# The factors of the last layer norm's last two batches: from POOL's power to ACT's square root with a Heron step on DVE, and the last batch scaled by DVE

## The reference

```
def _layernorm(x, axis=-1, eps=1e-05):
    m = jnp.mean(x, axis=axis, keepdims=True)
    v = jnp.var(x, axis=axis, keepdims=True)
    return (x - m) / jnp.sqrt(v + eps)

x = _layernorm(x + attention(x))
x = _layernorm(x + clip(x + moe(x), -100, 100))     # the change is in this norm
```

## Time and profile before

| | |
|---|---|
| median of 3 runs | 480.27 us (479.36 to 481.34) |
| the profiled execution's own time | 484.16 us |
| its span, first to last instruction | 482.4 us |
| last stage, first load of results to the end | about 446.8 to 482.4 us |
| ACT's scaling of batches 4 to 7 | 471.12 to 477.38 us |

### The profile page before, as it was taken

The page is one execution under the profiler, slowest core; times in us unless marked ns, Lnnn a source line. Parts: engine busy times, 40 slices in busy tenths (PEclk is TensorE's granted clock), DMA queues, the critical chain, the costliest instruction groups (busy, mean ns, idle before and its releaser), DMA issues.

```text
span 482.4 us, 20473 instructions
## 1 busy us (share of the span) xinstructions
PE 404.3 (84%) x8282; PEld 264.5 (55%) x8282; DVE 374.5 (78%) x995; ACT 326.8 (68%) x778; POOL 278.3 (58%) x443
## 2 busy tenths in 40 slices
PE   8598999899999998998999889789588988794860
PEld 2354446445455555545545545337487877693760
DVE  7887669989999999999998999877977665630381
ACT  5175675786886877777787667675788887770055
POOL 7022332535746747656655666786777777777173
PEclk9989899999999999999999999999799999997995
DMA  6648378745455365265264241133444433320753
GB/s 186 170 119 251 104 233 243 204 143 148 114 168 167 96 182 167 86 196 168 86 195 148 81 124 49 32 85 103 118 131 107 111 95 88 86 76 22 225 190 109
DMA packets 77500, 65.18 MB, mean 135 GB/s; under 512 B 12102, under 2 KB 71757, under 8 KB 77408
## 3 DMA queue, kind: packets, MB, share of 16 engines
q1 hardware_dynamic: 68240, 55.01, 39.1%
q0 software_dynamic: 4512, 8.54, 5.5%
q10 hardware_dynamic: 4656, 0.34, 0.7%
HBM read 36.88 MB, written 25.46 MB: 129 GB/s over the span
## 4 chain that ended last, share of the span: by engine, by line
PE 34%; ACT 18%; DVE 16%; DMA 12%; issue 8%; POOL 5%; SPq 4%; ACTq 3%; POOLq 0%; DVEq 0%
ACT probs L808 11%; PE psum L1038 10%; PE psum L951 10%; DVE nmax L1351 8%; PE psum L985 5%; POOL o_dram L759 4%; DMA o_dram<-probs,xs 4%; DMA experts<-o_dram 3%; DMA xs<-xs_dram 3%; ACTq L853 2%; PE psum L1210 2%; PE psum L1193 2%; ACT k L820 2%; DMA qst<-nmrows 2%; SPq L421 1%
## 5 line engine op out<-in xcount | busy, mean ns | idle before, releaser
L808 ACT ACTIVATE probs<-psum 128x512 f32<-128x512 f32 x320 | 180.3, 598 | 58.6 <-PE psum L951 47.4
L1351 DVE TENSOR_REDUCE nmax<-psum 128x2 f32<-128x1024 f32 (+7 forms) x256 | 181.4, 748 | 25.6 <-PE psum L998 25.2
L691 POOL TENSOR_SCALAR_AFFINE_SELECT probs<-probs 128x512 f32<-128x512 f32 x186 | 84.3, 484 | 113.1 <-ACT probs L808 112.4
L951 PE MATMUL psum<-qst,kst 128*32 128x512 bf16 (+3 forms) x2048 | 121.8, 303 | 18.8 <-ACT probs L808 14.3
L985 PE MATMUL psum<-kst,qst 128*32 128x512 bf16 (+7 forms) x2048 | 99.7, 290 | 4.1 <-DVE nmax L1351 2.6
L759 POOL DMA_INDIRECT o_dram<-probs,xs x77 | 78.2, 1016 | 26.5 <-issue 18.6
L951 PEld LDWEIGHTS psum<-qst,kst 128*32 128x32 bf16 x2048 | 44.0, 96 | 78.7 <-ACT probs L808 58.6
L1038 PE MATMUL psum<-probs,vst 128*32 128x512 f32 (+3 forms) x1024 | 80.9, 436 | 0.0
L998 PE MATMUL psum<-bmask,bident 128*32 128x64 bf16 (+2 forms) x1280 | 66.0, 200 | 1.0 <-issue 1.0
L985 PEld LDWEIGHTS psum<-kst,qst 128*32 128x32 bf16 x2048 | 47.2, 97 | 21.9 <-DVE nmax L1351 4.7
L998 PEld LDWEIGHTS psum<-bmask,bident 128*32 128x32 bf16 x1280 | 35.1, 98 | 14.8 <-issue 1.5
(11 more groups left out here) (221 smaller groups left out, 655.4 us busy)
## 6 DMA issues: line engine op xcount, KB each, us to landing
kst<-dk SPq DMA_DIRECT2D x62, 128.0 KB, 2.9
qst<-dq SPq DMA_DIRECT2D x31, 256.0 KB, 3.6
xs<-xs_dram SPq DMA_DIRECT2D x77, 66.0 KB, 1.9
experts<-o_dram SPq DMA_DIRECT2D x7, 512.0 KB, 4.7
dk<-k SPq DMA_DIRECT2D x7, 384.0 KB, 3.7
dq<-q SPq DMA_DIRECT2D x7, 384.0 KB, 2.7
xT_sb<-in_xT SPq DMA_DIRECT2D x8, 256.0 KB
xTv_sb<-in_xT SPq DMA_DIRECT2D x8, 256.0 KB, 3.7
```

The lines of the kernel that those rows point to most:

```text
L691: pool.affine_select(out=view, in_=view, compare_op=ALU.is_ge, fill=0.0, base=0, pattern=[[0, view.shape[1]], [1, P]], channel_multiplier= ...
L808: act.activation(probs[:, c % 2, p, kk * T:(kk + 1) * T], ps_t[:, k % 2, :], ACT.Exp, scale=SCALE).then_inc(S["exp_done"], 1)
L951: last = pe.matmul(out[32 * g:32 * g + 32], stationary[:, 32 * g:32 * g + 32], moving, skip_group_check=True, **flags)
L1351: last = dve.tensor_reduce(nmax[:, c, 2 * t:2 * t + 2], ps[:, :, at:at + TWO * (t + 1)], AX.X, ALU.max, negate=True)
```

## The change

The batches 6 and 7 (`LEFT = 2`) leave POOL's table `SPREADS`. Their factors are made together, for 8 numbers in each partition. With v = variance + eps, DVE writes v / 4 (`fin_var`), ACT takes its square root r (`fin_root`), and DVE does one Heron step for the square root of v: `fin_std` = (v / 4) / r + r, with a reciprocal and a product for the quotient. A second reciprocal gives `fin_rs`, and one more instruction `fin_off`. ACT then scales batch 6 as before, and DVE scales batch 7 with 4 `tensor_scalar` instructions. SP stores both batches in halves, in the order 7 first half, 6 first half, 7 second half, 6 second half. An activation with the square root on one column is added ahead of the last stage. Some semaphores are merged (`fin_moments` for `fin_stats` and `fin_aggr`, `fin_terms` for `fin_rstd`), and `fin_ready` now rises at every activation.

```diff
--- before.py
+++ after.py
@@ -47,6 +47,7 @@
 
     B1_AT, W2_AT, B2_AT, WCOLS = F, F + FC, 2 * F + FC, 2 * F + FC + D
     FIN = 4
+    LEFT, LINKS = 2, 6
     NT = NTOK * TOPK // P + E - 1
 
 
@@ -204,6 +205,11 @@
         fin_st = sb("fin_st", [P, 2, NQ, 6])
 
         fin_mv = sb("fin_mv", [P, 4, NQ, 2])
+        fin_root = sb("fin_root", [P, LEFT, NQ])
+        fin_var = sb("fin_var", [P, LEFT, NQ])
+        fin_inv = sb("fin_inv", [P, LEFT, NQ])
+        fin_quot = sb("fin_quot", [P, LEFT, NQ])
+        fin_std = sb("fin_std", [P, LEFT, NQ])
         fin_rs = sb("fin_rs", [P, 4, NQ])
         fin_off = sb("fin_off", [P, 4, NQ])
 
@@ -227,7 +233,7 @@
             top_link hot_ready rank_link pos_ready slot_ready
             gate_exp first_link tab_link free_known tables_ready padded gate_link 
             xsT_filled xsT_copied w_copied h_filled gelu_done y_filled y_copied
-            diag_ready summed clipped residual_pool residual_dve fin_stats fin_aggr fin_terms fin_rstd fin_off
+            diag_ready summed clipped residual_pool residual_dve fin_moments fin_terms fin_off fin_rooted fin_last
             fin_ready
             """.split()}
         ITEMS = ("ot", "q", "k", "va", "vb", "on", "woa", "wob", "rk")
@@ -390,7 +396,7 @@
         DVE_AHEAD = 4
 
 
-        SPREADS = ((0, 1), (2, 3), (4, 5), (6,), (7,))
+        SPREADS = ((0, 1), (2, 3), (4, 5))
         POOL_ADDS = {0: 0, 2: 0, 4: 1}
         TAIL_STEPS = {"pe": 12, "act": 12, "dve": 13}
         TABLE_STEP = 13
@@ -603,13 +609,15 @@
 
                     sp.wait_ge(o_loaded[q - 2], 16)
                 load_results(q, range(NQ), o_loaded[q])
-            for q in range(B - 1):
-                sp.wait_ge(S["fin_ready"], 2 * q + 2)
+            for q in range(B - LEFT):
+                sp.wait_ge(S["fin_ready"], NQ * (q + 1))
                 store_results(q, range(NQ))
             for half in range(2):
-                sp.wait_ge(S["fin_ready"], 2 * (B - 1) + half + 1)
+                sp.wait_ge(S["fin_last"], LINKS + 2 * half + 2)
                 store_results(B - 1, (2 * half, 2 * half + 1))
-            sp.wait_ge(out_stored, 16 * (B + 1))
+                sp.wait_ge(S["fin_ready"], NQ * (B - 2) + 2 * half + 2)
+                store_results(B - 2, (2 * half, 2 * half + 1))
+            sp.wait_ge(out_stored, 16 * (B + 2))
 
 
         @block.gpsimd
@@ -773,17 +781,17 @@
             def spread(n):
                 these = SPREADS[n]
                 at, count = these[0] % 4, len(these)
-                pool.wait_ge(S["fin_aggr"], NQ * (these[-1] + 1))
+                pool.wait_ge(S["fin_moments"], 2 * NQ * (these[-1] + 1))
                 if these[0] >= 4:
 
-                    pool.wait_ge(S["fin_ready"], 2 * (these[-1] - 3))
+                    pool.wait_ge(S["fin_ready"], NQ * (these[-1] - 3))
                 rs, off, mv_of = (t[:, at:at + count] for t in (fin_rs, fin_off, fin_mv))
                 pool.tensor_scalar(rs, mv_of[:, :, :, 1], EPS, None, ALU.add).then_inc(S["fin_terms"], 1)
                 pool.tensor_scalar(off, mv_of[:, :, :, 0], -1.0, None, ALU.mult).then_inc(S["fin_terms"], 1)
-                pool.wait_ge(S["fin_terms"], 2 * n + 2)
+                pool.wait_ge(S["fin_terms"], 3 * n + 2)
                 pool.tensor_tensor(rs, rs, mhalf[:].unsqueeze(1).to_broadcast([P, count, NQ]), ALU.pow
-                                   ).then_inc(S["fin_rstd"], 1)
-                pool.wait_ge(S["fin_rstd"], n + 1)
+                                   ).then_inc(S["fin_terms"], 1)
+                pool.wait_ge(S["fin_terms"], 3 * n + 3)
                 pool.tensor_tensor(off, off, rs, ALU.mult).then_inc(S["fin_off"], 1)
 
             for n in range(len(SPREADS)):
@@ -933,14 +941,22 @@
                 if DIAG_FROM <= j < DIAG_FROM + B * TOPK * NQ:
                     diagonal(j - DIAG_FROM)
 
-            for q in range(B):
+            act.activation(fin_root[:, 0, 0:1], k_ones[:], ACT.Sqrt)
+
+            def scale_rows(q, rows):
+                for n in rows:
+                    at = xr[:, q * T + P * n:q * T + P * n + P]
+                    act.activation(at, at, ACT.Identity, bias=fin_off[:, q % 4, n:n + 1], scale=fin_rs[:, q % 4, n:n + 1]
+                                   ).then_inc(S["fin_ready"], 1)
+
+            for q in range(B - LEFT):
                 act.wait_ge(S["fin_off"], 1 + [q in these for these in SPREADS].index(True))
-                for n in range(NQ):
-                    rows = xr[:, q * T + P * n:q * T + P * n + P]
-                    last = act.activation(rows, rows, ACT.Identity, bias=fin_off[:, q % 4, n:n + 1],
-                                          scale=fin_rs[:, q % 4, n:n + 1])
-                    if n % 2:
-                        last.then_inc(S["fin_ready"], 1)
+                scale_rows(q, range(NQ))
+                if q == B - LEFT - 1:
+                    act.wait_ge(S["fin_last"], 1)
+                    act.activation(fin_root[:], fin_var[:], ACT.Sqrt).then_inc(S["fin_rooted"], 1)
+            act.wait_ge(S["fin_last"], LINKS)
+            scale_rows(B - 2, range(NQ))
 
 
         @block.tensor
@@ -1712,18 +1728,37 @@
                     else:
                         dve.wait_ge(S["residual_dve"], g + 1 - sum(p < g for p in POOL_ADDS))
                     if g >= 2:
-                        dve.wait_ge(S["fin_aggr"], NQ * (g - 1))
+                        dve.wait_ge(S["fin_moments"], 2 * NQ * (g - 1))
                     for n in range(NQ):
-                        dve.bn_stats(fin_st[:, g % 2, n, :], xr[:, g * T + P * n:g * T + P * n + P]).then_inc(S["fin_stats"], 1)
+                        dve.bn_stats(fin_st[:, g % 2, n, :], xr[:, g * T + P * n:g * T + P * n + P]).then_inc(S["fin_moments"], 1)
                     if g >= 4:
 
                         dve.wait_ge(S["fin_off"], 1 + [g - 4 in these for these in SPREADS].index(True))
                     for n in range(NQ):
-                        dve.wait_ge(S["fin_stats"], NQ * g + n + 1)
-                        dve.bn_aggr(fin_mv[:, g % 4, n, :], fin_st[:, g % 2, n, :]).then_inc(S["fin_aggr"], 1)
+                        dve.wait_ge(S["fin_moments"], 2 * NQ * g + n + 1)
+                        dve.bn_aggr(fin_mv[:, g % 4, n, :], fin_st[:, g % 2, n, :]).then_inc(S["fin_moments"], 1)
                 if q < B and q not in POOL_ADDS:
                     dve.wait_ge(S["clipped"], q + 1)
                     dve.tensor_tensor(rows, rows, fin[:, q % FIN, :], ALU.add).then_inc(S["residual_dve"], 1)
+
+            dve.wait_ge(S["fin_moments"], 2 * NQ * B)
+            two = slice((B - LEFT) % 4, (B - LEFT) % 4 + LEFT)
+            dve.tensor_scalar(fin_var[:], fin_mv[:, two, :, 1], 0.25, EPS / 4, ALU.mult, ALU.add).then_inc(S["fin_last"], 1)
+            dve.wait_ge(S["fin_rooted"], 1)
+            link = linker(S["fin_last"], 1)
+            link(dve.reciprocal(fin_inv[:], fin_root[:]))
+            link(dve.tensor_tensor(fin_quot[:], fin_var[:], fin_inv[:], ALU.mult))
+            link(dve.tensor_tensor(fin_std[:], fin_quot[:], fin_root[:], ALU.add))
+
+            dve.wait_ge(S["fin_ready"], NQ * (B - 4))
+            link(dve.reciprocal(fin_rs[:, two], fin_std[:]))
+            link(dve.scalar_tensor_tensor(out=fin_off[:, two], in0=fin_mv[:, two, :, 0], scalar=-1.0, in1=fin_rs[:, two],
+                                          op0=ALU.mult, op1=ALU.mult))
+            q = B - 1
+            for n in range(NQ):
+                rows = xr[:, q * T + P * n:q * T + P * n + P]
+                dve.tensor_scalar(rows, rows, fin_rs[:, q % 4, n:n + 1], fin_off[:, q % 4, n:n + 1], ALU.mult, ALU.add
+                                  ).then_inc(S["fin_last"], 1)
 
 
 # ---- launch: one core; the host transposes weights and activations, nothing else ----
```

## The result

The change makes the kernel 0.5% faster: the median of 20 runs went from 480.37 to 477.87 us, the ratio is 0.9947 (95% interval 0.9929 to 0.9965). One of the 20 executions of the changed kernel took 1343.9 us and is left out of the ratio. The prediction said 480.2 us and no change, so 2.5 us are to be explained.

What follows compares the result with a forecast made beforehand. The prediction took ACT's activations as the bound of the last stage. Its terms, -1.54 + 1.37 + 0.11 = -0.06 us, turned 480.27 into 480.2 us, no change, with a range of 479.1 to 481.4 us.

Steps and rivals of the forecast that it cites:

- The step that failed: End of the span, behind the last store's landing: 3.2 us, with SP waiting 2.9 us, taken as fixed and untouched.
- The removal is worth nothing by itself: POOL's last two factor calls go; batch 7's were ready 0.60 us before ACT needed them, so no gain.
- ACT's count: Last stage on ACT: four activations of batch 7 go at 0.385 us each, 1.54 us less.
- the round trip: Batch 6's factors from ACT's square root through DVE and back to ACT: 1.37 us, between 1.20 and 1.82.
- The stores: Four 128 KB halves at the end: SP's extra issuing hidden by 0.01 us, last store held up 0.11 us by bytes.
- DVE's scaling: Batch 7's four instructions on DVE, at most 0.28 us each, end near 476.6 us, hidden ahead of ACT's batch 6.
- The table load: One new 1.28 us load behind ACT's last GELU, hidden in 30.26 us of ACT idle time.
- The rivals: Last stage: short round trip, 480.0 us (0.20); long one, up to 480.65 us (0.22); table loads inside it, 482.8 us (0.02).
- something unseen: Unnamed causes anywhere, chance 0.06, half on each side and not all of it beyond 0.5%.

Runs made afterwards that it cites:

- e5_before_drain: Kernel before the change plus one POOL DRAIN behind its last indirect DMA, ahead of the last stage; ratio 0.9953, 477.33 against 480.49 us.
- e1_late_pool: Changed kernel plus a one-column POOL memset at its end that waits for DVE's last factor; ratio to the kernel before 1.001, 480.73 against 480.49 us.
- e4_act_queue: Changed kernel with the last half of batch 6 stored from ACT's queue instead of SP's; profile only, 18.0 us from last load's issue to end.
- e6_after_drain: Changed kernel plus the same early POOL DRAIN ahead of the last stage; ratio to the kernel before 0.9948, 478.26 against 480.33 us.

## Why the prediction was wrong

**The step that failed** is in its first part: "From 479.2 to the end of the span at 482.4 us there are 3.2 us, in which SP waits for the other engines' end (2.9 us)", and then "The change touches none of that, and I take it as fixed." The row was read, its size was right, and the question what SP waited for was not asked. It was for POOL's DRAIN, which ended 7.0 us behind the end of POOL's last instruction in all eight profiles without an early DRAIN, and the change moves that instruction: from 475.14 - 462.0 = 13.1 us behind the mark to 468.45 - 459.3 = 9.2 us. Of the 3.2 us, 2.7 were to be had: without the DRAIN the span would have ended 0.4 us behind the landing at 479.3 us, and e5_before_drain came to 17.8 us from the mark in place of 20.4.

**"The removal is worth nothing by itself"** (POOL's two last calls) is wrong for the same reason. That POOL's factors were ready 0.60 us before ACT came to them was right, but POOL had a second customer, the end of the program. The removal is the only part of the change that gains: e5_before_drain has the gain without the rest, e1_late_pool has the rest without the gain.

**ACT's count and the round trip** were right. The saving of 1.54 us was paid back by 1.31 us. The small instructions measured 203 ns (reciprocal, forecast 0.20), 168 and 166 (products, 0.16), 166 (`fin_off`, 0.165) and 191 (square root, 0.20). The Trainium skill's figures ("VectorE: DVE Perf Modes", under the fixed hardware budget) had led to an estimate of 0.15 us for the reciprocal; the trace says 0.203, so between 8 and 32 columns it grows by (353 - 203) / 24 = 6.3 ns a column and not by 8.3. The measurement decides.

**The stores** were under-charged. Forecast: 0.11 us late. The last landing came 476.9 - 474.53 = 2.4 us behind ACT's end, and 1.8 us before: 0.55 us more. SP has a part in it: of four issues in a row the last three cost it 0.469 to 0.492 us each, not 0.372, and the last one began 0.44 us behind ACT, where 0.02 was forecast. The row of that issue in the changed kernel:

```profile
L601 SPq DMA_DIRECT2D out<-xr x1: 492/492/492, 475.0 to 475.0; - x1
...
DMA to landing us min/median/max: 2.0/2.0/2.0
```

The bytes were slower as well: the four halves moved at 249 GB/s, not 296, as this stretch shows (the last three numbers are PEclk, DMA share, GB/s):

```profile
474.40:476.50 2.10, 0.00 (x0) 0.00 (x0) 0.00 (x0) 0.12 (x1) 0.00 (x0) 0.50 0.86 249
```

The engines weren't full in it (0.86), and a half of 131 KB every 0.53 us, which is how SP issued the last ones, is 247 GB/s too, so this rate can be SP's doing. But e4_act_queue took SP's lateness at the last store away, and the landing still came 2.3 us behind ACT's end. How the 0.55 us divide between SP and the bytes isn't shown. So without the drain the change is 1.54 - 1.31 - 0.55 = -0.3 us, a small loss, in keeping with what e6_after_drain (18.0) against e5_before_drain (17.8) shows. The forecast of about nothing for the parts that it looked at was right in kind; DVE's scaling (0.34 us an instruction, one every 0.26 us, 1.11 us in all) was hidden as said.

**The table load** was hidden as said. ACT behind its last GELU in the changed kernel:

```profile
428.16 0.63 ACT L922 ACTIVATE hT_sb<-psum,kst 128x128 f32<-128x128 f32 x2
428.81 1.28 ACT L944 ACT_TABLE_LOAD   x1
430.10 0.20 ACT L944 ACTIVATE fin_root<-k_ones 128x1 f32<-128x1 f32 x1
```

The load starts 0.02 us behind the GELU and costs 1.28 us, with no drain around it; the Trainium skill ("ScalarE: Activation LUTs", on what a table load costs) has 1.28 us for the load, which agrees, and 1.38 us of drain, which this trace doesn't show.

**The rivals.** None of the named ones came true, and none of them named the mechanism that did. The 0.03 for faster by over 0.5% stood for "something unseen"; the wait of 2.9 us was printed in the prediction's own evidence, under PE's name, and the rows of the DRAINs weren't.

## What to carry to other kernels

The end of a program is a race between all engines' closing work, so before a wait at the end is called fixed, open the rows of the line that closes it and see which DRAIN ends last and when it could have begun. For an engine that issued indirect DMAs, as POOL here, either try to have its last instruction early or give it a DRAIN of its own in an idle stretch; each was worth about 0.5% here. An engine that is ahead of its customers in the work may still be last at the barrier; work taken from it at the end is worth the time by which its last instruction moves, up to the next event that ends last, and two ways of moving it don't add.

## What was not expected of the hardware

- POOL's closing DRAIN takes 7.28 us here (7.14 to 7.40 us in the eight profiles without an early one, where it started with POOL's last instruction and ended 7.0 us behind it); in the kernel before DVE's, ACT's and PE's take 0.28 to 2.2 us, which is about their last work. POOL's falls to 0.303 us when another DRAIN ran behind the last indirect DMA, and grows by 0.082 us for each indirect DMA issued since, as measured at 20, 60 and 68. The early DRAINs follow the same line at 73 and 81 and lie some 55 DMAs below it at 121 and 141. The Trainium skill ("VectorE: DVE Perf Modes", on the DRAIN that can't be avoided) says of the DRAINs that the runtime puts around a kernel that they are constant at about 12 ns on all five engines. These here carry a line of the kernel, so they may be others: SP's closing one is 13 ns, near that figure, and POOL's is 7.28 us.
- POOL's DRAIN at the start of the program took 0.17 us, so 7.28 us is no constant of that engine.
- Four stores of 128 KB issued in a row by SP cost it 0.37 us for the first and 0.47 to 0.49 us for each of the others. Moving the last one to ACT's queue gave an issue 0.03 us behind the work, and a landing at most 0.1 us earlier.
